# Bank sums of a fused group-norm and batch-norm kernel: six adds a unit moved from VectorE to ScalarE and GpSimd

## What is computed

```python
def _gn(v, G=32, eps=1e-5):            # 2 channels a group
    m, s = mean and variance over the group's channels and pixels, per image
    return (v - m) / sqrt(s + eps)

g = _gn(x)
m = g.sum(axis=1) != 0                 # per image and pixel, over all 64 channels
mean, var = per channel, over the batch's places where m holds (with padding)
out = x + where(m, g / sqrt(var + 1e-3), g)    # place (0, 0) treated apart
```

## Time and profile before

| | |
|---|---|
| median of 3 runs | 1297.34 us (1297.0 to 1297.68) |
| the profiled execution | 1296.76 us, span 1294.7 us, 10367 instructions |
| busy: PE, DVE, ACT, POOL | 719.7, 920.1, 714.9, 306.3 us |
| HBM read and written | 268.44 MB each, 415 GB/s over the span |
| mean granted TensorE clock | 0.752 of full speed |

### The profile page before, as it was taken

The page is one execution under the profiler, slowest core; times in us unless marked ns, Lnnn a source line. Parts: engine busy times, 40 slices in busy tenths (PEclk is TensorE's granted clock), DMA queues, the critical chain, the costliest instruction groups (busy, mean ns, idle before and its releaser), DMA issues. The chain is left out here.

```text
span 1294.7 us, 10367 instructions
## 1 busy us (share of the span) xinstructions
PE 719.7 (56%) x2882; PEld 321.0 (25%) x2882; DVE 920.1 (71%) x2078; ACT 714.9 (55%) x764; POOL 306.3 (24%) x324
## 2 busy tenths in 40 slices
PE   0666644566445664456644466544665446654476
PEld 0322312222222222122222222222222122222232
DVE  7888667687676766767767677676776776766774
ACT  0666544665446654466544566445664456644565
POOL 0033222232222322123222232222222222312220
PEclk9977767777678776687766787667876678866778
DMA  9999999999999999999999999999999999999996
GB/s 380 415 421 420 421 420 421 421 421 421 421 421 421 420 422 420 421 422 420 421 421 420 421 421 420 421 420 421 421 418 421 419 418 420 421 421 416 418 411 272
DMA packets 135466, 537.56 MB, mean 415 GB/s; under 512 B 4336, under 2 KB 4336, under 8 KB 135408
## 3 DMA queue, kind: packets, MB, share of 16 engines
q1 hardware_dynamic: 69936, 276.83, 52.3%
q10 hardware_dynamic: 65472, 260.05, 48.9%
HBM read 268.44 MB, written 268.44 MB: 415 GB/s over the span
## 5 line engine op out<-in xcount | busy, mean ns | idle before, releaser
L480 DVE BATCH_NORM_STATS2 stats<-slots 128x6 f32<-128x512 f32 x1024 | 639.2, 680 | 192.8 <-DMA slots<-in_x_dram 191.4
L355 ACT ACTIVATE slots<-slots,out_bias,out_scale 128x1024 f32<-128x1024 f32 x512 | 604.3, 1235 | 62.3 <-PE flush L430 53.9
L430 PE MATMUL flush<-slots,weights 128*64 128x512 f32 x1536 | 424.4, 689 | 0.0
L334 POOL TENSOR_TENSOR sums<-fresh,sums 128x512 f32<-128x512 f32 x180 | 229.9, 1277 | 511.5 <-ACT fresh L352 511.5
L494 DVE SCALAR_TENSOR_TENSOR sums<-flush,group_bias,sums 128x512 f32<-128x512 f32 x180 | 133.2, 740 | 128.5 <-PE flush L430 128.5
L430 PEld LDWEIGHTS flush<-slots,weights 128*64 128x64 f32 x1536 | 149.0, 156 | 215.4 <-issue 213.7
L367 ACT ACTIVATE by_image<-by_image,eps 128x16 f32<-128x16 f32 x32 | 9.8, 307 | 329.6 <-DVE by_image L517 329.6
L311 POOL TENSOR_TENSOR weights<-pair_sum,group_rstd 128x256 f32<-128x256 f32 (+1 forms) x128 | 73.3, 604 | 439.2 <-DVE group_bias L530 439.2
L395 PE MATMUL small_ps<-stats,group_avg 128*128 128x64 f32 x64 | 22.1, 444 | 255.2 <-DVEq L506 255.2
L426 PE MATMUL stay<-slots,weights 128*64 128x512 f32 x512 | 139.1, 600 | 0.0
L427 PE MATMUL stay<-minus_mean,weights 128*64 128x512 f32 x512 | 138.2, 593 | 0.0
(11 more groups left out here) (54 smaller groups left out, 254.0 us busy)
## 6 DMA issues: line engine op xcount, KB each, us to landing
slots<-in_x_dram SPq DMA_DIRECT2D x127, 2048.0 KB, 19.3
out_dram<-slots ACTq DMA_DIRECT2D x124, 2048.0 KB, 29.6
out_dram<-slots SPq DMA_DIRECT2D x16, 512.0 KB, 5.1
slots<-in_x_dram SPq DMA_DIRECT2D x4, 512.0 KB, 15.1
```

The costliest lines, as they stand in the source:

```text
L334: pool.tensor_tensor(into, fresh[:, n % FRESH_BUFS, :], into, ALU.add).then_inc(added_by_pool, 1)
L355: nc.scalar.activation(out_in_ring(u, i), image_in_ring(u, i), ACT.Identity, bias=out_bias[:, u % 2, i:i + 1], scale=out_scale[:, u % 2, i ...
L430: nc.tensor.matmul(into, weight, source, start=True, stop=True).then_inc(image_summed, 1)
L480: last = V.bn_stats(stats[:, u % 2, k * BLOCK_STATS:(k + 1) * BLOCK_STATS], source)
```

## The change

VectorE adds no sums any more. All twelve banks of a unit that don't stay are read by ScalarE and added by GpSimd, as the six odd ones were; the three buffers between them stay three. The semaphore `added` now counts GpSimd's adds, `taken` all twelve reads of a unit, and the last unit's comparisons on VectorE count on a semaphore of their own, `compared`. The order of ScalarE's instructions is as before: the read of an image's bank, then its output.

```diff
-    by_dve = flushed[0::2]
-    by_pool = flushed[1::2]
-    ADDS_BEFORE = {8: by_dve[0:3], 14: by_dve[3:4], 16: by_dve[4:5], 20: by_dve[5:6]}
...
         def taken_with(u, i):
-            return u * len(by_pool) + by_pool.index(i) + 1
+            return u * len(flushed) + flushed.index(i) + 1
...
-            if u == LAST or i in by_dve:
-                engine.wait_ge(added, added_with(u, i))
+            if u < LAST:
+                engine.wait_ge(taken, taken_with(u, i))
             else:
-                engine.wait_ge(taken, taken_with(u, i))
+                engine.wait_ge(compared, flush_order(u).index(i) + 1)
...
                 if 0 < u < LAST:
-                    for i in by_pool:
+                    for i in flushed:
                         n = taken_with(u - 1, i) - 1
                         pool.wait_ge(taken, taken_with(u, i))
                         if u > 1:
-                            pool.wait_ge(added_by_pool, taken_with(u - 2, i))
+                            pool.wait_ge(added, taken_with(u - 2, i))
                         into = sums[:, flushed.index(i), :]
-                        pool.tensor_tensor(into, fresh[:, n % FRESH_BUFS, :], into, ALU.add).then_inc(added_by_pool, 1)
+                        pool.tensor_tensor(into, fresh[:, n % FRESH_BUFS, :], into, ALU.add).then_inc(added, 1)
...
-                    if u < LAST and i in by_pool:
+                    if u < LAST and i in flushed:
                         take(u, i)
...
-            def add_sums(u, i):
-                at = flushed.index(i)
-                share = group_bias[:, u % 2, i:i + 1]
-                wait_for_sum(dve, u, i)
-                if u == 0:
-                    V.tensor_scalar(sums[:, at, :], bank_of(u, i), share, None, ALU.add).then_inc(added, 1)
-                else:
-                    dve.wait_ge(added, added_with(u - 1, i))
-                    V.scalar_tensor_tensor(out=sums[:, at, :], in0=bank_of(u, i), scalar=share, in1=sums[:, at, :],
-                                           op0=ALU.add, op1=ALU.add).then_inc(added, 1)
...
                 for k in range(AHEAD if u else 0, UNIT_BLOCKS):
-                    if u:
-                        for i in ADDS_BEFORE.get(k, ()):
-                            add_sums(u - 1, i)
                     block_stats(u, k)
...
-                    if i in by_dve:
-                        dve.wait_ge(added, added_with(LAST - 1, i))
-                    else:
-                        dve.wait_ge(added_by_pool, taken_with(LAST - 2, i))
+                    dve.wait_ge(added, taken_with(LAST - 2, i))
```

More of the change, by code:

```diff
@@ L164, in norm_conv_kernel @@
         image_summed = sem("image_summed")
+        taken = sem("taken")
         added = sem("added")
-        taken = sem("taken")
-        added_by_pool = sem("added_by_pool")
+        compared = sem("compared")
         out_ready = sem("out_ready")
@@ L211, in bank_of @@
             return flush[(u * ADDS + flush_order(u).index(i)) % FLUSH_BANKS][:, :]
-        def added_with(u, i):
-            return u * len(by_dve) + (flush_order(u) if u == LAST else by_dve).index(i) + 1
         def taken_with(u, i):
-            return u * len(by_pool) + by_pool.index(i) + 1
+            return u * len(flushed) + flushed.index(i) + 1
         def wait_for_bank(engine, u, i):
-            if u == LAST or i in by_dve:
-                engine.wait_ge(added, added_with(u, i))
+            if u < LAST:
+                engine.wait_ge(taken, taken_with(u, i))
             else:
-                engine.wait_ge(taken, taken_with(u, i))
+                engine.wait_ge(compared, flush_order(u).index(i) + 1)
         def wait_for_all_stores(engine):
@@ L350, in take @@
                     if n >= FRESH_BUFS:
-                        act.wait_ge(added_by_pool, n + 1 - FRESH_BUFS)
+                        act.wait_ge(added, n + 1 - FRESH_BUFS)
                 nc.scalar.activation(into, bank_of(u, i), ACT.Identity, bias=group_bias[:, u % 2, i:i + 1]).then_inc(taken, 1)
@@ L576, in count @@
                 else:
-                    if i in by_dve:
-                        dve.wait_ge(added, added_with(LAST - 1, i))
-                    else:
-                        dve.wait_ge(added_by_pool, taken_with(LAST - 2, i))
+                    dve.wait_ge(added, taken_with(LAST - 2, i))
                     V.scalar_tensor_tensor(out=not_zero[:, i, :], in0=bank_of(LAST, i), scalar=group_bias[:, LAST % 2, i:i + 1],
                                            in1=sums[:, flushed.index(i), :], op0=ALU.subtract, op1=ALU.not_equal,
-                                           accum_out=n_part[:, i:i + 1]).then_inc(added, 1)
+                                           accum_out=n_part[:, i:i + 1]).then_inc(compared, 1)
             dve.wait_ge(stored[NOT_ZERO_TILE % RING], 16 * (NOT_ZERO_TILE // RING + 1))
@@ L588, in _ @@
             dve.wait_ge(counted, len(kept))
-            dve.wait_ge(added, LAST * len(by_dve) + ADDS)
+            dve.wait_ge(compared, ADDS)
             V.tensor_reduce(n_row, n_part[:, :], AX_X, ALU.add).then_inc(small_in, 1)
```

## The result

| | before | after |
|---|---|---|
| median of 22 runs each | 1297.05 us (1296.64 to 1297.87) | 1294.93 us (1294.41 to 1295.42) |
| profiled execution, its span | 1296.76, 1294.7 us | 1294.88, 1293.2 us |
| mean granted TensorE clock | 0.752 | 0.775 |

The ratio is 0.9983, with a 95% interval of 0.9977 to 0.9989: 2.1 us or 0.17% less. Something that the prediction priced at 0.1 gave 2 us.

The account below looks back on a forecast made before the run. One lagging DMA engine was taken as the bound. Six terms of 0 and 0.1 us for fetches took the profiled 1296.76 to 1296.9, 1297.4 as a median (0.6 above), range 1295.6 to 1299.8.

Parts of the forecast that it names:

- The bound: At the end of the run, one lagging DMA engine sets the time; its work is bytes, which the change doesn't move.
- Instruction fetches: Over the whole program, at most some 350 more instructions, 23 KB to fetch by DMA: +0.1 us, at most 0.9.
- VectorE: 0: Inside the run, VectorE loses six adds a unit, 137 us busy, but then waits longer for loads: 0.
- ScalarE: 0: Six more reads a unit, 4.1 us, delay stores by 1.4 to 4.1 us, covered by 15 us of waiting: 0.
- Two signs: If right, ScalarE's fourth store is no longer held for 4 us, and the first store's 25.0 us becomes about 23.6.
- GpSimd: 0: Six more adds a unit at 1.277 us fit between reads 1.86 us apart, so ScalarE never waits: 0, bound 7.7 a unit.
- TensorE: 0: Sums wait for banks read by ScalarE and end about 1213, before TensorE's next work at 1217.95: 0.
- the clock rival: TensorE's clock stays low through a unit's sums, 42.8 us a unit: +71 us, 1369. Chance 0.03.
- First unit: 0: The same stage starts with four stores owed and loads still coming: 0, at most 1.4 us.
- Last unit: 0: VectorE's 4.4 us gain is lost to ScalarE, first store 0.5 us later, covered by the lagging engine's old work: 0.
- The rival of a faster end: The end follows the last unit, not the lagging engine, so VectorE's 4.4 us come off: 1292.9. Chance 0.04.
- The lap: The two-unit lap of stores, loads and engines is the bound; 15 laps grow by 3.4 us: +51, 1348. Chance 0.06.

Follow-up runs that it names:

- 1: The changed kernel with 12 more VectorE instructions a unit, semaphore increments that touch no tensor: 1296.83 us, ratio 0.9999 to the kernel before.
- 2: The changed kernel with 24 more VectorE semaphore increments a unit, 720 in all: 1301.04 us, ratio 1.003 to the kernel before.
- 3: The changed kernel with 12 more ScalarE semaphore increments a unit, ahead of outputs with a bank read: 1295.0 us, ratio 0.9984 to the kernel before.
- 5: The changed kernel with every second ScalarE bank read made twice, six more a unit: 1294.35 us, ratio 0.9979 to the kernel before.
- 6: The changed kernel with all twelve ScalarE bank reads of a unit made twice: 1337.23 us, ratio 1.0309 to the kernel before.
- 4: The changed kernel with seven more bn_stats on VectorE ahead of the last unit's last block: 1294.46 us, ratio 0.9981 to the kernel before.
- 9: The changed kernel with three of 128 tiles stored as 120 and 8 partitions: 1301.58 us, in two groups, 1297 to 1298 and 1301 to 1302.
- 11: The kernel before, its VectorE adds kept, with three fewer VectorE instructions a unit, 96 in all: 1296.64 us, ratio 0.9997.

## Why the prediction was wrong

**The bound** was read rightly: one lagging DMA engine sets the end, and the run has a lone engine at its end before and after. "Its work is the bytes, and the change moves none" was wrong. The working took the lag as given and didn't ask what it came from. The trace of before held the answer: 16.2 us of lag, built up in steps of 1 us at the fetches.

**Instruction fetches** is the step that failed: "I take 0.1, as nothing ties them to it". They are tied to it (the steps, and 1 and 2 against 3), and what it put at +0.1 was -2.1. Two things went wrong in that term. It counted the program's instructions, which rise by 325 (10367 to 10692), so its sign was a cost; but the engine carries VectorE's, which fall by 366 (2407 to 2041). And it priced a fetch by its bytes. 8 KB at the 29 GB/s of a lone engine is 0.28 us, and the packet's own time in the trace is 0.31 us, but the engine is delayed by 0.9 to 1.0. With the right count and price the term is -3 x 1.0, and the forecast about 1294.3. Why a packet of 0.31 us delays the engine by three times as much was not shown.

**VectorE: 0.** Right in its sense: the work taken away gave nothing (1 has it taken away and no gain). Its instructions gave the 2.1 us (in 1 they come back to within 0.2 us, with an interval of about 1.2 us either way).

**ScalarE: 0.** Right (5, 6), though the delays were put too high. A unit's stage after takes 25.1 us from 1189.29 to the fourth store at 1214.42, against 22.5, so the fourth is late by 2.6, not 4.1 (the first three by 0.3, 0.9 and 2.0, not 1.4, 2.7 and 3.4): an output and a read together take 1.70 us, not 1.86, since each begins before the one ahead has ended. ACT in unit 29:

```profile
1189.88 1.23 ACT L346 ACTIVATE slots<-slots,out_bias,out_scale 128x1024 f32<-128x1024 f32 x1
1191.01 0.67 ACT L343 ACTIVATE fresh<-flush,group_bias 128x512 f32<-128x512 f32 x1
1191.58 1.23 ACT L346 ACTIVATE slots<-slots,out_bias,out_scale 128x1024 f32<-128x1024 f32 x1
...
1195.68 0.38 ACTq L352 DMA_DIRECT2D out_dram<-slots  x1
...
1214.42 2.91 ACTq L352 DMA_DIRECT2D out_dram<-slots  x1
1222.50 0.31 ACT L358 ACTIVATE by_image<-by_image,eps 128x16 f32<-128x16 f32 x1 [8.11 <-DVE by_image L495]
```

Two signs that the prediction named came out otherwise. The fourth store is still held, 2.91 us in place of 4.06. And the first store, issued at 1195.68, took 26.2 us, not 23.6: the whole stage began 3.1 us sooner, after a load that landed sooner, and it landed 1.6 us sooner, so it stood the longer behind older ones. The root still finds ScalarE free, by 8.11 us.

**GpSimd: 0.** Right. Its adds, 1.27 us, have 1.70 us each; ScalarE never waited for one.

**TensorE: 0,** and the clock rival: right. Sums of unit 29:

```profile
1187.20 5.21 PE L421 MATMUL flush<-slots,weights 128*64 128x512 f32 x12
...
1204.32 1.08 PE L421 MATMUL flush<-slots,weights 128*64 128x512 f32 x4 [0.62 <-ACT fresh L343]
1206.02 1.08 PE L421 MATMUL flush<-slots,weights 128*64 128x512 f32 x4 [0.62 <-ACT fresh L343]
...
1214.80 0.69 PE L386 MATMUL small_ps<-stats,group_avg 128*128 128x64 f32 x2 [5.95 <-DVEq L484]
```

The waits for banks came, 0.62 us each, in the last tile. They took 1.9 us of the 7.87 that TensorE had idle ahead of its small products. The sums ended 21.6 us behind their start (22.7 forecast). The clock stayed at 1.00 (2.4 GHz) through the waits: in the stretches of 4 us from 1193 to 1209 the granted clock is 1.00 in each, and over the span it is 0.775, more than before. The two with the waits:

```profile
1201.00:1205.00 4.00, 3.38 (x17) 0.86 (x13) 3.75 (x7) 4.00 (x5) 2.03 (x2) 1.00 1.02 419
1205.00:1209.00 4.00, 3.22 (x14) 0.95 (x12) 0.00 (x0) 4.00 (x6) 2.02 (x3) 1.00 1.03 422
```

The Trainium skill, "TensorE: Matmul & The Clock Gate", section "A second HAM failure mode: psum-queue depth-cycling", tells of a kernel in which brief idle times between groups of products made the clock fall and rise; here waits of 0.62 us did not.

**First unit: 0.** Nothing speaks against it; the first slice is 378 GB/s against 380.

**Last unit: 0.** The sum was right, its inside wrong. The forecast was a first store 0.5 us later, at 1267.1, since ScalarE would hold the root until 1260.25. It came at 1262.42. Unit 30's outputs had begun sooner, as every stage since the lag was smaller, and ScalarE was done at 1255.5; VectorE, no longer behind, waited for the last load, which landed 3.1 us sooner. The cover that was named (old work on the lagging engine) hid this gain as it would have hidden the loss (4).

**The chances.** The rival of a faster end at 1292.9 lay 2.0 us off the result, hardly nearer than the forecast (2.5), and its mechanism is refuted by 4. The lap, at 1348, doesn't decide with six reads more, nor with twelve (5); with eighteen (6) ScalarE itself does. The range's own terms don't give its ends: 0.9, 1.4 and half a microsecond above 1297.4 are 1300.2, not 1299.8, and its -1.2 has no source. The result lies below either way.

**What stays open.** In the profiled pair the last load landed 3.1 us sooner (1250.03 against 1253.13), but the stores behind it 2.3 and the end 1.6. Some 0.8 to 1.5 us was given back while the engines emptied their queues; over the medians it is 2.1 of 3. Why was not shown. Nor was which of the 16 engines it is, nor what makes the second slowest lag (6.9 us behind the middle one on the store of 1204.19, 7.9 after), nor the spread of 9, nor the small size of 11.

## What to carry to other kernels

Where transfers bound a kernel, look at the slowest DMA engine, not at the mean: compare, on some transfers, when the last of the 16 parts lands and when the middle one does, and ask what the lag grows with. If it grows in steps, see which engine's instruction fetches stand at the steps: here each 128 instructions of VectorE, waits and semaphore instructions included, cost 0.8 us (14 to 19 fetches) to 1.0 us (14 to 22) of a run in which VectorE was idle 38% of the time. Merge them, drop waits that another wait covers, or hand them to an engine whose fetches make no steps (ScalarE and GpSimd here), and price the work that goes along by its own cover.

## What the runs showed that I had not expected

- Each of VectorE's instruction fetches delays the DMA engine that ends last by 0.9 to 1.0 us, three times the packet's 0.31 us. ScalarE's don't (twelve instructions a unit more: 1295.0 against 1294.93).
- Stores cut into 120 and 8 partitions are slow: 26 issues in place of 16 took SP until 1293.1, with the transfers at 211 GB/s, and behind a tile cut so the next load into its slot went out 1.4 to 1.7 us late.
- VectorE beside an add of GpSimd. In the last unit's statistics after, one small operation with two inputs took 1.32 us, before 0.24:

```profile
1252.66 0.22 DVE L490 TENSOR_TENSOR spread<-dev 128x64 f32<-128x64 f32 x1
1252.92 1.32 DVE L491 SCALAR_TENSOR_TENSOR spread<-stats,spread 128x64 f32<-128x64 f32 x1
```

```profile
1252.89 1.27 POOL L325 TENSOR_TENSOR sums<-fresh,sums 128x512 f32<-128x512 f32 x1 [0.44 <-ACT fresh L343]
```

It ended 0.08 us behind GpSimd's add, which had begun 0.03 us before it. The Trainium skill, "SBUF — State Buffer", section "SBUF: two separate sides", says that a VectorE operation with two SBUF inputs and a GpSimd operation that reads SBUF need the same pair of ports, and that the one which starts first keeps the other out for its whole length. This trace agrees, at 1.1 us for one operation. Here VectorE had time for it. A chain of small operations that is on the critical path would not.
